# Output biases on ScalarE ahead of time, residual adds from PSUM, the mixing stage in key-first order, and fewer filler products in four norms

## The reference

```python
x = x + tanh(g_xattn[n]) * attention_n(layernorm(x), ctx)
x = x + tanh(g_ffn[n])   * feed_forward_n(layernorm(x))
```

```python
out = attn @ Wp.T + bp          # layer 0; Wo, bo in layers 1 to 3
out = out * mask_t              # layer 3 only
```

```python
xr = mu_r * x + (1.0 - mu_r) * x_prev
xk = mu_k * x + (1.0 - mu_k) * x_prev
r = sigmoid(xr @ W_r.T)
k = xk @ W_k.T
out = r * (square(relu(k)) @ W_v.T)
```

## Time and profile before

| What | us |
|---|---|
| median of 3 runs | 526.56 |
| fastest, slowest of them | 523.25, 532.5 |
| the profiled execution | 520.9 |
| its span, first to last instruction | 519.1 |
| PE, DVE, ACT, POOL busy | 451.7, 288.3, 221.9, 110.3 |
| mean granted TensorE clock | 0.987 |

### The profile page before, as it was taken

The page is one execution under the profiler, slowest core; times in us unless marked ns, Lnnn a source line. Parts: engine busy times, 40 slices in busy tenths (PEclk is TensorE's granted clock), DMA queues, the critical chain, the costliest instruction groups (busy, mean ns, idle before and its releaser), DMA issues.

```text
span 519.1 us, 7751 instructions
## 1 busy us (share of the span) xinstructions
PE 451.7 (87%) x3062; PEld 277.2 (53%) x3062; DVE 288.3 (56%) x597; ACT 221.9 (43%) x441; POOL 110.3 (21%) x97
## 2 busy tenths in 40 slices
PE   6999999888999877987888998989879689958986
PEld 4434433545765534766645775864345445645552
DVE  3756775365455564786245654635477744366461
ACT  2345574211311354444243334533457445727370
POOL 1200000210101002543000005002164450880400
PEclk9999999899999999999999999999999799989999
DMA  8700000630000000000000010000111010111000
GB/s 305 289 1 1 2 1 0 251 83 1 1 1 0 1 0 2 0 2 2 1 0 0 2 54 28 3 0 0 21 20 23 0 21 16 27 21 21 5 18 20
DMA packets 5493, 16.16 MB, mean 31 GB/s; under 512 B 1490, under 2 KB 2387, under 8 KB 4947
## 3 DMA queue, kind: packets, MB, share of 16 engines
q1 hardware_dynamic: 5458, 15.68, 9.8%
HBM read 13.06 MB, written 0.52 MB: 26 GB/s over the span
## 4 chain that ended last, share of the span: by engine, by line
PE 62%; DVE 17%; ACT 6%; POOL 6%; issue 5%; DMA 2%; SPq 1%; DVEq 0%; ACTq 0%; POOLq 0%
PE PS L527 54%; PE PS L781 2%; PE PS L1128 2%; DVE mx L1726 2%; DVE wmoe L1719 2%; DVE mxd L2130 1%; ACT wmoe L1559 1%; DVE hp L1669 1%; DMA den<-wmoe 1%; POOL wmoe L2355 1%; DVE keys L1838 1%; ACT PT L1388 1%; POOL wmoe L2378 1%; POOL den L2375 1%; PE PS L609 1%
## 5 line engine op out<-in xcount | busy, mean ns | idle before, releaser
L2329 POOL TENSOR_TENSOR rstd<-veps,mhalf 128x4 f32<-128x4 f32 x16 | 16.5, 1039 | 248.3 <-DVE veps L1663 248.3
L527 PE MATMUL PS<-PTB,keys 128*64 128x128 f32 (+3 forms) x384 | 41.9, 383 | 0.0
L1559 ACT ACTIVATE wmoe<-PS,mxd 128x512 f32<-128x512 f32 (+3 forms) x64 | 33.1, 533 | 3.3 <-DVE mxd L2130 3.2
L1838 DVE TENSOR_REDUCE keys<-PS 128x9 f32<-128x693 f32 x32 | 26.5, 871 | 8.6 <-PE PS L527 8.6
L1571 ACT COPY PTB<-PS 128x768 f32<-128x768 f32 (+1 forms) x24 | 20.9, 870 | 23.6 <-PE PS L1128 23.3
L527 PE MATMUL PS<-cst 128*128 128x512 f32 (+1 forms) x64 | 30.8, 597 | 0.0
L527 PE MATMUL PS<-keys,PTB 32*128 32x231 f32 (+2 forms) x448 | 27.1, 327 | 3.8 <-DVE wmoe L1719 2.7
L2375 POOL TENSOR_TENSOR den<-den,cst 128x1024 f32<-128x1024 f32 x7 | 16.5, 2354 | 64.2 <-DMA den<-wmoe 64.2
L527 PEld LDWEIGHTS PS<-PTB,keys 128*64 128x64 f32 (+2 forms) x384 | 21.5, 149 | 14.7 <-issue 11.3
L527 PE MATMUL PS<-va,PT 128*128 128x72 f32 (+2 forms) x224 | 28.0, 276 | 1.0 <-ACT PT L1388 1.0
L527 PEld LDWEIGHTS PS<-va,PT 128*128 128x128 f32 (+1 forms) x224 | 26.4, 191 | 2.8 <-ACT PT L1388 2.0
(11 more groups left out here) (348 smaller groups left out, 946.6 us busy)
## 6 DMA issues: line engine op xcount, KB each, us to landing
wmoe<-w_dram SPq DMA_DIRECT2D x2, 2048.0 KB, 11.4
den<-wmoe SPq DMA_DIRECT2D x28, 64.0 KB, 2.3
wa<-wa_dram SPq DMA_DIRECT2D x4, 256.0 KB, 5.5
wlate<-ew_dram SPq DMA_DIRECT2D x2, 512.0 KB, 4.8
wd<-wd_dram SPq DMA_DIRECT2D x1, 1024.0 KB, 9.0
wlate<-wm_dram SPq DMA_DIRECT2D x1, 1024.0 KB, 5.1
cst<-const_dram SPq DMA_DIRECT2D x1, 754.5 KB, 6.9
cst<-const_dram SPq DMA_DIRECT2D x1, 551.0 KB, 5.0
```

Source lines behind the costliest of these rows:

```text
L527: return nc.tensor.matmul(o, l, r, start=start, stop=stop, skip_group_check=True)
L1559: A_(PR[n % 2][:, z, to:to + (t + 1) * 128], PS[:, ring_banks("turn", n).start + z, to:to + (t + 1) * 128], ACT.Exp, bias=mxd[:, n % 2, k, ...
L1838: last = v.tensor_reduce(mxn[:, 2 * half + t, :].rearrange("p (g r) -> p g r", r=32)[:, :, 12:15], PS[:, at:at + NG, t * 256:t * 256 + GK] ...
L2329: g.tensor_tensor(rstd[:, b, :], veps[:, b, :], mhalf[:], ALU.pow).then_inc(S("ln_rstd"), 1)
```

## The change

Three things are changed.

1. **Output biases.** In layers 0, 1 and 2, ACT adds `tanh(gate) * bias` to `x` in SBUF (`biased`, 128x512, once for each sequence), at a point between the norm that read `x` and the residual: after the second part of units 2 and 3 in layer 0, after the squares of norm 2 in layer 1, and at the end of units 0 and 1 in layer 2. The product of tanh and bias is made by small ACT instructions of one column. DVE then adds `x` and the projection from PSUM in one instruction, and the ACT pass of L1442, L1497 and L1365 is gone. In layer 3 the bias can't go ahead of the mask, so DVE does both steps: `(PS + bias) * mask` into `yb`, and then the residual. The semaphores `y_placed` are gone; PE waits for `x_ready` in their place. In layer 0 the first sequence's add stands ahead of `take(6)` on DVE.
2. **The mix.** ACT makes a sigmoid of one column right after the squares of norm 3, so that the table is loaded there. The key's operands, products and relus come ahead of the receptance's.
3. **Fillers.** In norms 2, 3, 4 and 6 `keep_clock(512, 256)` ahead of both spreads becomes `keep_clock(256)` between the two.

```diff
             def layernorm(i):
                 for part in (ln_centre, ln_variance, ln_spread):
-                    if part is ln_spread:
-                        pe.wait_ge(S("ln_act"), 4 * i + 2)
-                        keep_clock(centre_bank(i, 0), 512, 256)
                     for b in range(B):
+                        if part is ln_spread and b == 1:
+                            pe.wait_ge(S("ln_act"), 4 * i + 2)
+                            keep_clock(centre_bank(i, 0), 256)
                         part(i, b)
...
-                            pe.wait_ge(S("l0_y_placed"), 1)
+                            pe.wait_ge(S("x_ready"), 1)
                         turn_sums(u - 1)
...
                         elif j == 2 and u == 3:
-                            pe.wait_ge(s_("y_placed"), before(a, "y_placed") + 1)
+                            pe.wait_ge(S("x_ready"), 2 * i + 1)
...
-                pe.wait_ge(s_("y_placed"), before(a, "y_placed") + B)
+                pe.wait_ge(S("x_ready"), 2 * i + 2)
...
                 for b in range(B):
-                    pe.wait_ge(S("mix_in"), 2 * b + 1)
+                    pe.wait_ge(S("mix_in"), b + 1)
+                    mm(PS[:, 5 + 2 * b, :], wf1[:, 1, :], sq[:, b, :]).then_inc(S("mix_up"), 1)
+                for b in range(B):
+                    pe.wait_ge(S("mix_in"), B + b + 1)
                     mm(PS[:, 4 + 2 * b, :], wf1[:, 0, :], xc[:, b, :]).then_inc(S("mix_up"), 1)
-                    pe.wait_ge(S("mix_in"), 2 * b + 2)
-                    mm(PS[:, 5 + 2 * b, :], wf1[:, 1, :], sq[:, b, :]).then_inc(S("mix_up"), 1)
-                for b in range(B):
                     pe.wait_ge(S("mix_k2"), b + 1)
                     mm(PS[:, 2 * b, :], wf1[:, 2, :], att[:, b, :]).then_inc(S("mix_v"), 1)
...
+            def biased(b, column, made_, done):
+
+                act.wait_ge(S("bias_scaled"), made_)
+                A_(xb[b], xb[b], ACT.Identity, bias=small[:, column:column + 1]).then_inc(S(done), 1)
...
-                def project(b):
-                    act.wait_ge(s_("projected"), before(a, "projected") + b + 1)
-                    A_(yb[:, b, :], PS[:, 7, :], ACT.Identity, bias=small[:, 11 + a:12 + a]).then_inc(s_("y_placed"), 1)
...
+                    if a == 1 and u < B:
+                        biased(u, 10, 3, "at_biased")
...
             def linear():
                 layernorm(2)
                 for b in range(B):
+                    biased(b, 15, 2, "lin_biased")
...
                 for b in range(B):
-                    act.wait_ge(S("lin_proj"), b + 1)
-                    act.wait_ge(S("lin_att"), b + 1)
-                    A_(yb[:, b, :], PS[:, 6 + b, :], ACT.Identity, bias=V("bo1")).then_inc(S("lin_y"), 1)
...
                 layernorm(3)
-                for b in range(B):
-                    act.wait_ge(S("ln_h"), 2 * 3 + b + 1)
-                    for mu, dst in ((0, xc), (1, sq)):
+                A_(small[:, 8:9], small[:, 6:7], ACT.Sigmoid)
+                for mu, dst in ((1, sq), (0, xc)):
+                    for b in range(B):
+                        act.wait_ge(S("ln_h"), 2 * 3 + b + 1)
...
                 def add(b):
-                    dve.wait_ge(s_("y_placed"), before(a, "y_placed") + b + 1)
+                    dve.wait_ge(s_("projected"), before(a, "projected") + b + 1)
                     if a == 2:
-                        link(v.tensor_tensor(yb[:, b, :], yb[:, b, :], mask3f[:, b * T:(b + 1) * T], ALU.mult))
-                    residual(b, layer)
+                        link(v.scalar_tensor_tensor(yb[:, b, :], PS[:, 7, :], small[:, 13:14], mask3f[:, b * T:(b + 1) * T],
+                                                    ALU.add, ALU.mult))
+                        residual(b, layer)
+                    else:
+                        dve.wait_ge(S("at_biased"), b + 1)
+                        residual(b, layer, PS[:, 7, :])
...
+                mixed(1, 0)
+                mixed(1, 1)
+                mixed(0, 0)
+                squared(0)
+                mixed(0, 1)
+                squared(1)
                 for b in range(B):
                     dve.wait_ge(S("mix_v"), b + 1)
+                    dve.wait_ge(S("mix_act"), B + b + 1)
                     link(v.tensor_tensor(yb[:, b, :], yb[:, b, :], PS[:, 2 * b, :], ALU.mult))
                     residual(b, 5)
```

More of the change, by code:

```diff
@@ L156, in signals @@
                 turned_keys=parts, by_dve=units * own, by_act=parts - units * own,
-                weighed=units, o_taken=units, turned=B, att_done=B, projected=B, y_placed=B)
+                weighed=units, o_taken=units, turned=B, att_done=B, projected=B)
 def copied(a, u, j):
@@ L731, in attention0 @@
                 keep_clock(2, 512, 512)
-                pe.wait_ge(S("l0_y_placed"), B)
+                pe.wait_ge(S("x_ready"), B)
             def attention(a, i, w):
@@ L1413, in attention @@
                                 half_weights(u + 1, half)
-                    step()
-                    if s == nsub - 1:
-                        todo += [nothing]
-                        todo += [lambda b=b: project(b)]
-                    if b == 1 and u + 1 < len(units):
-                        step()
+                    if a == 1 and u < B:
+                        biased(u, 10, 3, "at_biased")
                 ln_squares(i + 1, 0)
-                while todo:
-                    step()
             def attention0():
@@ L1438, in root @@
                     A_(rmsr[:, b, :, :], rms[:, b, :].rearrange("p (t n) -> p t n", t=TB), ACT.Sqrt).then_inc(S("l0_rms_r"), 1)
-                def project(b):
-                    act.wait_ge(S("l0_projected"), b + 1)
-                    A_(yb[:, b, :], PS[:, 7, :], ACT.Identity, bias=V("bp")).then_inc(S("l0_y_placed"), 1)
                 layernorm(0)
@@ L1643, in _ @@
             A_(tg[:], V("g"), ACT.Tanh).then_inc(S("gates"), 1)
+            act.wait_ge(S("gates"), 1)
+            for n, name in enumerate(("bp", "bo1")):
+                A_(small[:, 14 + n:15 + n], V(name), ACT.Identity, scale=tg[:, n:n + 1]).then_inc(S("bias_scaled"), 1)
             act.wait_ge(S("lam_dots"), 2)
@@ L1680, in widen, with residual @@
                                      src.unsqueeze(3).to_broadcast([128, TB, n, width]))
-            def residual(b, gate):
-                v.scalar_tensor_tensor(xb[b], yb[:, b, :], tg[:, gate:gate + 1], xb[b], ALU.mult,
+            def residual(b, gate, of=None):
+                v.scalar_tensor_tensor(xb[b], yb[:, b, :] if of is None else of, tg[:, gate:gate + 1], xb[b], ALU.mult,
                                        ALU.add).then_inc(S("x_ready"), 1)
@@ L1887, in add @@
                 def add(b):
-                    dve.wait_ge(S("l0_y_placed"), b + 1)
-                    residual(b, 0)
+                    dve.wait_ge(S("l0_projected"), b + 1)
+                    dve.wait_ge(S("l0_biased"), b + 1)
+                    residual(b, 0, PS[:, 7, :])
                 dve.wait_ge(S("l0_keys"), 1)
@@ L1913, in attention0 @@
                         maxima(u + 2, 0)
+                    if u == 7:
+                        add(0)
                     if u > 0:
@@ L1919, in attention0 @@
                         scale(0)
-                    elif u == 7:
-                        add(0)
                 take(NU - 1)
```

40 lines of the change are left out of this document (19 added, 21 removed).

## The result

| | before | after |
|---|---|---|
| median, us | 526.70 | 529.68 |
| mean, us | 528.37 +/- 1.16 | 530.02 +/- 0.98 |
| lowest to highest, us | 521.32 to 536.64 | 522.87 to 536.62 |
| executions | 20 | 20 |
| profiled execution: time, span, us | 520.9, 519.1 | 525.42, 523.4 |

After stands to before as **1.0088, 95% interval 1.0045 to 1.0131**: 0.9% slower, where 0.6% faster was forecast. The means and clocks are over all executions except three beyond 600 us (two of before, one of an experiment).

A forecast was written before the change was run, and what follows sets the result against it. The prediction took the chain of waits, mostly through PE, to bound the kernel. Terms of -3.95 us and +0.85 for the clock made -3.1, so 517.8 for the profiled 520.9 and 523.4 on the median, range 518 to 529.5.

The forecast's parts named there:

- What bounds the kernel: Whole kernel: chain of waits through PE for 62% of the span, DVE 17%, ACT 6%.
- The fillers: -0.45, -0.73, -0.79: Norms 2, 4 and 6: spreads no longer wait behind PE's fillers, saving 0.45, 0.73 and 0.79 us.
- Norm 3 and the mix: -2.19: Norm 3 to norm 4's second centring: 2.19 us sooner, 1.28 from the table and 0.66 from the norm.
- The rival in which half is given back: Mix gains only 1.3 us, norms 1.0, as PE's products queue and norms wait on POOL; 525.3 us, chance 0.14.
- ACT's bias pass gone: -0.73 and -0.38: DVE's residual starts without ACT's copy: 0.73 us at the linear part's end, 0.38 at layer 2's attention end.
- The bias passes that come in: 0: Six ACT passes of 0.72 us in layer 0, norm 2 and layer 2 fit idle time; at most 0.2 each.
- Layer 3: +0.83 and +0.49: PE waits for DVE's two steps: last unit's keys 0.83 us later, the heads' first product 0.49 later.
- The rival "more": Layer 3's two waits cost nothing and the clock holds: -5.27 us, or 521.2 us; chance 0.11.
- The clock: +0.85: PE's clock in the changed norms: half of one full fall more than before, 0.85 us, bounds none and three.
- The prediction's own sign of being wrong: Profile after: more than two new stretches at 0.50 clock would show the forecast wrong.
- The slower rival: Norms 2 to 6 and mix: fillers held the clock, three more falls cost 5.13 us; +1.2, 527.8 us; chance 0.15.

The follow-up runs named there:

- E9: The changed kernel with 256 filler columns ahead of each spread of norms 2, 3, 4 and 6; mean 523.57 us, ratio 1.0013.
- E3: The kernel before with the bias changes alone, old fillers and old mix; mean 531.78 us, ratio 1.0044.
- E11: E6 with PE's layer 3 waits on DVE's first step, as in E7; mean 524.41 us, ratio 0.9955.
- E7: The changed kernel with bank 7 freed by the first of DVE's two steps in layer 3, not the residual; mean 530.52 us, ratio 1.0051.
- E1: The kernel before with the change to the fillers of norms 2, 3, 4 and 6 alone; mean 529.27 us, ratio 1.0083.
- E5: The changed kernel without any filler in norms 2, 3, 4 and 6; mean 532.41 us, ratio 1.0179.
- E12: The kernel before with 256 filler columns ahead of each spread in place of 512 and 256 ahead of both; mean 523.93 us, ratio 0.9972.
- E6: The changed kernel with 256 filler columns ahead of each spread and 512 between norm 3 and the mix; mean 523.40 us, ratio 1.0005.
- E4: The changed kernel with the old fillers of 512 and 256 columns ahead of both spreads again; mean 528.91 us, ratio 1.0110.
- E8: The changed kernel with the old fillers, 512 filler columns between norm 3 and the mix, and E7's edit; mean 526.66 us, ratio 1.0024.

## Why the prediction was wrong

**What bounds the kernel** was read rightly: the chain lost ACT's part and kept PE and DVE.

The difference was forecast to be under 2%, with a chance of 0.94, and it is; its direction was forecast wrongly, and the median of 529.68 lies above the 518 to 529.5 that were given.

**The fillers: -0.45, -0.73, -0.79.** Like by like, they gave -0.24, -0.66 and -0.73. In norm 2 (E9, full clock) the second spread ends 0.71 behind POOL, before 0.95. In norms 4 and 6 the first product starts 0.61 and 0.60 behind POOL's second power, before 1.27 and 1.33; the rows of after are these:

```profile
197.06 1.98 POOL L2332 TENSOR_TENSOR rstd<-veps,mhalf 128x4 f32<-128x4 f32 x2 [11.55 <-DVE veps L1650]
...
199.65 3.67 PE L527 MATMUL PS<-hp,keys 128*128 128x512 f32 x8
...
313.36 1.98 POOL L2332 TENSOR_TENSOR rstd<-veps,mhalf 128x4 f32<-128x4 f32 x2 [49.57 <-DVE veps L1650]
...
315.94 2.39 PE L527 MATMUL PS<-hp,keys 128*128 128x512 f32 x5
```

The term was put too high because four transposes were taken at 0.45, where a row of four is listed with 0.65: the old end of 165.93 had the tail of the last transpose in it and the new one had not. In norms 4 and 6 the product starts 0.61 and 0.60 behind the power, where 0.54 stood.

**Norm 3 and the mix: -2.19.** It gave -1.90, with the table in the wait ahead of `hp` and no drain. Of the 0.29 that is missing 0.23 is there when DVE's first `hp` starts, 1.75 behind POOL's start where 1.52 stood: it is the transposes again. From 187.76 the six products of the mix follow one another as laid out, the last from 192.15 (the profile lists each f32 product twice). The rival in which half is given back falls.

**ACT's bias pass gone: -0.73 and -0.38.** In the linear part DVE takes the projection at 179.58 and PE centres at 180.39, with no copy between: -0.72, the start of ACT's copy to DVE's residual in the earlier trace rows. At the end of layer 2 `hp` starts 0.69 behind the spread's start (E9: 249.84 and 250.53), before 1.06: -0.37. The residual took its operand from PSUM at the old price:

```profile
179.58 1.61 DVE L1670 SCALAR_TENSOR_TENSOR x<-PS,tg,x 128x512 f32<-128x512 f32 x2 [0.37 <-PE PS L527]
```

**The bias passes that come in: 0.** Six on ACT, 728 ns each, none with idle time ahead of it, and neither the sum of the terms nor a row of PE has a cost for them. Right as far as it shows, though at equal clock E3 is 0.8 +/- 0.5 us above before, where its terms give +0.3. The group of after by shape (busy us, mean ns, idle before):

```profile
L1353 ACT ACTIVATE x<-x,small 128x512 f32<-128x512 f32 x6 | 4.2, 728 | 0.0
```

**Layer 3: +0.83 and +0.49.** 1.59 - 0.74 = +0.85 and 3.41 - 2.85 = +0.56. In E11 the keys start 0.81 behind the step (341.78 and 340.97) and the heads' first product 2.63 behind its step (353.01 and 350.38), so both are out again; E7 is 1.7 us shorter than after at equal clock. The rival "more", in which they cost nothing, falls.

These terms sum to -3.21 where -3.95 stood, and the table has -3.2 to -3.6 at equal clock. That the chain gets some 3 us shorter was right.

**The clock: +0.85. This is the step that failed.** It was taken as "half of one full fall more than before", because no changed norm had fallen with the old fillers. After has a mean clock lower by 0.0105 than before, worth 0.0105 x 422 = 4.4 us, or about three stretches of 3.41: five times the term, and more than the chain gained. E1 has it from the fillers alone, E5 more of it with no filler, E9 and E12 take it back with fillers in another place, and norm 2 is where most of it lies (two to four stretches in all five traces with one filler or none). The prediction's own sign of being wrong, more than two new stretches at 0.50, came with five. The slower rival, that the fillers had held the clock and decide from three falls on, is what happened. Its +1.2 is what the chain and the clock give, -3.2 and +4.4, and what the means show (1.1 +/- 1.1 against the 94 of before, 1.7 +/- 1.5 against its own 20). The median rose by 3.0, which with 20 executions over 14 us doesn't contradict it, and the ratio's 0.9% is larger because the executions in it differ by more clock, 0.963 and 0.980.

The price of a stretch was well sized: up to 1.71 stood, and 1.4 was measured; what was mis-sized is how often the clock falls. Of the Trainium skill, "TensorE: Matmul & The Clock Gate", part 1 on the clock gate, the rule that TensorE is throttled by default and activity releases it was weighed and then given half a fall. The runs agree with it in kind: 0.966 with the old fillers, 0.956 with the new, 0.949 with none. They don't follow the amount: 512 columns to a norm, split, have 0.971 and 0.972 (E9, E12), more than 768 ahead of both.

The reason for the wrong size can be said: the full clock at four places in one execution was taken as their safety. That execution was at 0.987, and the mean of 94 is 0.966, so by 0.0033 for a stretch before has on average six stretches more than the trace that was read, which makes it a poor sample of its kernel. The three times of before, 523.25 to 532.5, said that already: 9 us between executions of one program are some six stretches, and the prediction took them as scatter without a cause.

**Open.** E7 has a lower clock than after (0.9506 +/- 0.0039 beside 0.9559 +/- 0.0023) and E11 than E6 (0.9655 +/- 0.0027 beside 0.9703 +/- 0.0021). Whether freeing the bank early costs clock, or both are chance, was not settled. The traces speak for chance: long falls in layer 3's attention begin at 334.6 in E3, 339.2 in E5 and 346.8 in E7, and all three begin ahead of the last unit's keys, the first work there that waits for the bank. Why 256 ahead of each spread holds better than 768 ahead of both wasn't measured by itself either; that it does is shown by the mean clock of E12 beside before, and by E9 beside E4 only in the same direction. How a filler in norm 2 bears on falls elsewhere isn't shown.

## What to carry over

A filler on TensorE is judged by the granted clock over many executions, not by whether the places around it ran at full clock in one trace. When a program's times scatter by 1 to 2%, set them against their clock first: here that gave a price for a lost stretch (1.4 us) and told a chain that got 3 us shorter from a clock that took 4 back. And compare traces of several kernels at the same place: one pair of traces had five new stretches, and only norm 2's two came back in every kernel with that order. Here a short filler ahead of each small dependent step, rather than long ones ahead of them all, cost the path little and held more; that is worth a try elsewhere, and shown for these norms.

## What the runs showed of the hardware

The clock can fall with little or no idle time listed on PE: 3.40 of 3.40 us busy ahead of the fall at 159.9 in E8, 6.54 of 6.78 ahead of that at 346.78 in E7, where PE did small operations, and 4.84 of 5.24 ahead of that at 166.24 in after. It also falls behind long waits (2.66 and 2.61 us in after), and the same waits in before passed at full clock. Once down it may stay so for long although PE is busy (13.46 of 13.65 us in E1, 18.85 of 20.48 in E7, 24.79 of 27.20 from 334.70 in E3). Executions of the kernel before have mean clocks between 0.947 and 0.990, and their times, 517 to 538 us, follow the clock with a correlation of -0.97: nearly all of the scatter is that. The load of the sigmoid's table took 1.28 us and the activation of one column followed with nothing between:

```profile
183.62 1.28 ACT L1483 ACT_TABLE_LOAD   x1
184.92 0.20 ACT L1483 ACTIVATE small<-small 128x1 f32<-128x1 f32 x1
```
